# An adaptive-norm transformer block on one core: feed-forward begun inside attention's end, and the key maxima three units ahead of the scores

## The reference

```python
mod = (silu(c) @ wmod).reshape(2, 6, 1, -1)
sa, ca, ga, sb, cb, gb = (mod[:, i] for i in range(6))    # ga, gb: kept at least 0.25 from zero
h = layernorm(x) * (1 + ca) + sa
x = x + ga * attention(h)      # 16 heads of 8; a token sees pages (32 tokens) up to its own
h = layernorm(x) * (1 + cb) + sb
x = x + gb * ffn(h)

# ffn: four rounds r, four experts e, the best two by logits
logits = cur @ Wg[r] + bg[r]
vals, idx = top_k(logits, 2)
cw = sum(one_hot(idx) * softmax(vals))                    # weight of each expert
hmid = gelu(einsum('nh,ehf->enf', cur, W1) + b1)
y = einsum('enf,efh->enh', hmid, W2) + b2
cur = cur + einsum('ne,enh->nh', cw, y)
```

## Time and profile before

| | |
|---|---|
| median of 3 runs | 743.12 us (735.27 to 758.76) |
| profiled execution, its device time | 735.29 us |
| its span | 733.5 us |
| PE / PEld | 661.3 us (90%) / 444.6 us (61%) |
| DVE | 570.4 us (78%) |
| ACT | 518.2 us (71%) |
| POOL | 177.9 us (24%) |
| mean granted clock of TensorE | 0.943 |

### The profile page before, as it was taken

One profiled execution on the slowest core, in us unless ns is written; L12 is line 12 of the kernel. 1 busy time (PEld: TensorE's weight loads), 2 busy tenths in 40 slices (PEclk: granted clock), 3 DMA queues, 4 the chain that ended last, 5 costly groups with the idle time before them and its releaser, 6 DMA issues.

```text
span 733.5 us, 11093 instructions
## 1 busy us (share of the span) xinstructions
PE 661.3 (90%) x4004; PEld 444.6 (61%) x4004; DVE 570.4 (78%) x951; ACT 518.2 (71%) x920; POOL 177.9 (24%) x154
## 2 busy tenths in 40 slices
PE   3936799999999989946999999999999999999996
PEld 2413344444444435535787778777877787778885
DVE  5577878888888864466789888888889888988775
ACT  2420077787787777634888888888888888888983
POOL 0232520000000000003244334442444244422222
PEclk9975589999999999966999999999999999999998
DMA  7288001011101000002111101110111011110200
GB/s 267 83 279 270 2 2 60 18 44 61 40 22 61 3 1 4 1 0 66 50 59 59 56 3 59 58 59 2 57 59 58 12 48 59 59 37 21 74 15 29
DMA packets 16902, 40.64 MB, mean 55 GB/s; under 512 B 2832, under 2 KB 8208, under 8 KB 14736
## 3 DMA queue, kind: packets, MB, share of 16 engines
q1 hardware_dynamic: 15536, 38.20, 15.3%
q10 hardware_dynamic: 1312, 1.74, 0.7%
HBM read 32.19 MB, written 9.57 MB: 57 GB/s over the span
## 4 chain that ended last, share of the span: by engine, by line
PE 35%; DVE 12%; issue 5%; ACT 1%; POOL 0%; POOLq 0%; DVEq 0%
DVE gel_lo L1027 7%; PE y L930 6%; PE y L932 6%; PE y L931 6%; PE hid L921 5%; PE hid L920 5%; PE hid L919 5%; PE plog L941 2%; DVE part L1083 1%; ACT gel_hi L995 1%; DVE at_least L1055 1%; PE pcw L950 1%; DVE cw L1074 0%; DVE cw L1072 0%; DVE dl L1062 0%
## 5 line engine op out<-in xcount | busy, mean ns | idle before, releaser
L1027 DVE TENSOR_TENSOR gel_lo<-gel,gel_hi 128x512 fp32r<-128x512 f32 x256 | 248.3, 1010 | 6.7 <-ACT gel_hi L995 5.7
L567 ACT ACTIVATE probs<-st 128x512 f32<-128x512 f32 (+1 forms) x320 | 160.4, 555 | 95.2 <-PE st L703 91.7
L599 DVE TENSOR_REDUCE mcol<-mx 128x2 f32<-128x1024 f32 (+2 forms) x160 | 176.7, 1118 | 38.5 <-PE mx L722 36.0
L994 ACT ACTIVATE gel<-hid,b_sb 128x512 f32<-128x512 f32 x256 | 176.1, 688 | 39.5 <-PE hid L921 17.1
L995 ACT ACTIVATE gel_hi<-hid,b_sb 128x512 fp32r<-128x512 f32 x256 | 174.8, 683 | 0.0
L1135 POOL TENSOR_TENSOR cur<-cur,part 128x512 f32<-128x512 f32 x64 | 106.5, 1663 | 251.3 <-DVE part L1083 251.3
L722 PE MATMUL mx<-ks,qs 30*128 30x128 f32 (+4 forms) x576 | 90.3, 392 | 22.5 <-PEq L228 13.3
L930 PE MATMUL y<-gel_hi,w_hi 128*128 128x512 f32 x256 | 104.6, 408 | 0.4 <-DVE gel_lo L1027 0.2
L919 PE MATMUL hid<-cur_hi,w_hi 128*128 128x512 f32 x256 | 102.5, 401 | 0.0
L920 PE MATMUL hid<-cur_lo,w_hi 128*128 128x512 f32 x256 | 102.3, 399 | 0.0
L921 PE MATMUL hid<-cur_hi,w_lo 128*128 128x512 f32 x256 | 102.2, 399 | 0.0
(11 more groups left out here) (140 smaller groups left out, 569.1 us busy)
## 6 DMA issues: line engine op xcount, KB each, us to landing
cwb<-gate_rows SPq DMA_DIRECT2D x16, 1024.0 KB, 4.7
ks<-k_rows SPq DMA_DIRECT2D x8, 512.0 KB, 3.7
qs<-q_rows SPq DMA_DIRECT2D x8, 512.0 KB, 4.8
q_rows<-pieces_q SPq DMA_DIRECT2D x12, 256.0 KB, 3.8
k_rows<-pieces_k SPq DMA_DIRECT2D x12, 256.0 KB, 4.5
x_sb<-in_x SPq DMA_DIRECT2D x4, 256.0 KB, 4.8
...
```

The costliest lines, as they stand in the source:

```text
L567: nc.scalar.activation(probs[k % PROBS][:, h, 0:n], st[:, (HG * k + h) % ST_RING, 0:n], ACT.Exp, scale=SCALE).then_inc(exp_done, 1)
L599: nc.vector.tensor_reduce(mcol[g % 2][:, PAIR_HEADS[pair]:PAIR_HEADS[pair] + 2, slot:slot + step * (len(blocks) - 1) + 1:step], mx[:, at % ...
L994: nc.scalar.activation(gel[n % RING][:, :], hid[n % RING][:, :], ACT.Gelu_apprx_tanh, bias=bias)
L1027: nc.vector.tensor_tensor(gel_lo[n % RING][:, :], gel[n % RING][:, :], gel_hi[n % RING][:, :], ALU.subtract).then_inc(lo_ok, 1)
```

## The change

1. `rstd_steps` and `root_step` are gone. `root_guess` (three VectorE instructions) makes a first guess of the inverse root from the bits of the number, and `root_refine` makes three Newton steps, 12 linked instructions, each waiting for the one before. In `prep` both are on VectorE; behind it the refinement and the scaling of the tiles are on GpSimd.
2. `LEAD` is 3 in place of 4, `TURN_AFTER` is one unit in place of two, and four bins change places.
3. Attention projects only 12 of the 16 tiles, with all of it ahead of the last `weigh`, and makes only chunk 0 of the feed-forward's input: GpSimd refines and scales, `normed` stands in the last unit, ScalarE's `hidden` between its exponentials, GpSimd cuts `cur`. It then also refines and scales chunk 1, `norm(1)`, in the same block.
4. The last four tiles, and the input of chunks 1 to 3, are made inside the feed-forward, between its steps 1 and 32, by tables of step numbers. The routing of chunks 0 to 4 has step numbers of its own.
5. `xn`, `rec`, `att`, `att_t` and the pieces of `cur` lie in memory that outlives the block; `cur_hi`, `cur_lo` and `cwb` take the place of `pieces` (so the order listings below name them pieces_q).

```diff
-LEAD = 4
-TURN_AFTER = 2 * PAIRS
+LEAD = 3
+TURN_AFTER = PAIRS
@@ BINS
+    ([(0, 0), (4, 512)], 128, 0, 12),
     ([(1, 0), (5, 512)], 256, 1, 12),
-    ([(0, 0), (4, 512)], 128, 0, 12),
     ([(5, 0)], 512, 5, 1),
+    ([(2, 256), (6, 768)], 128, 10, 4),
     ([(6, 0)], 512, 6, 1),
-    ([(2, 256), (6, 768)], 128, 10, 4),
@@
+def root_guess(nc, link, m, tiles):
+    ve, rstd, nw = m.ve[:, tiles, :], m.rstd[:, tiles, :], m.nw[:, tiles, :]
+    link(nc.vector.tensor_scalar(ve, m.mv[:, tiles, 1:2], EPS, None, ALU.add))
+    link(nc.vector.tensor_scalar(nw.bitcast(I32), ve.bitcast(I32), 1, None, ALU.arith_shift_right))
+    return nc.vector.tensor_scalar(rstd.bitcast(I32), nw.bitcast(I32), -1, ROOT_GUESS, ALU.mult, ALU.add)
+def root_refine(eng, link, m, tiles):
+    for _ in range(ROOT_STEPS):
+        link(eng.tensor_tensor(nw, rstd, rstd, ALU.mult))
+        link(eng.tensor_tensor(nw, nw, ve, ALU.mult))
+        link(eng.tensor_scalar(nw, nw, -0.5, 1.5, ALU.mult, ALU.add))
+        link(eng.tensor_tensor(rstd, rstd, nw, ALU.mult))
@@ attention, gpsimd
+            def norm(c):
+                pool.wait_ge(var_ok, c + 1)
+                root_refine(nc.gpsimd, link, m, chunk_tiles(c))
+                for t in range(TPC * c, TPC * (c + 1)):
+                    scaled(nc.gpsimd, m, xn, t).then_inc(xn_ok, 1)
+            norm(0)
+            pool.wait_ge(h_ok, 1)
+            nc.gpsimd.tensor_copy(m.cur_hi[:, 0, :], m.cur[:, 0, :]).then_inc(hi_ok, 1)
+            pool.wait_ge(hi_ok, 1)
+            nc.gpsimd.tensor_tensor(m.cur_lo[:, 0, :], m.cur[:, 0, :], m.cur_hi[:, 0, :], ALU.subtract).then_inc(cur_ok, 1)
+            norm(1)
@@ attention, tensor
+            for step in range(STEPS - FIRST_TILE, TILES + 2):
+                project(step)
             weigh(STEPS - 1)
-            pe.wait_ge(exp_done, HG * STEPS)
-            for step in range(STEPS - FIRST_TILE, NT + 2):
-                project(step)
-                if step == JB + 5:
-                    normed(0)
-                    normed(1)
-            normed(2)
-            normed(3)
@@ ffn
+    FIRST = 3 * TPC
+    TO_TOKENS = [6, 8, 12, 17]
+    DIVIDE = [7, 9, 13, 18]
+    BACK = [8, 14, 18, 22]
+    TURNED = [9, 15, 19, 23]
+    WO = [10, 16, 20, 24]
+    RESIDUAL = [11, 17, 21, 25]
+    GUESS = 26
+    FIRST_COMBINE = 6
+    NORMED = {1: 1, 2: 10, 3: 31}
+    HIDDEN = {1: 2, 2: 11, 3: 32}
+    START = {0: -1, 1: 4, 2: 15, 3: 33, 4: 44}
+    RANKS, TANH, WEIGHTS = (1, 3, 4, 5), 6, 7
@@ ffn, vector, ahead of step 0
+            for stage in range(len(RANKS)):
+                ranks(0, stage)
             low(0)
+            weights(0)
@@ ffn, gpsimd
+            norm(2)
+            parts(1)
             for k in range(CHUNKS):
                 for e in range(NE):
+                    accumulate(k, e)
+                    if (k, e) == (0, 2):
+                        parts(2)
+                    if (k, e) == (1, 1):
+                        norm(3)
+                if k == 1:
+                    parts(3)
+                    parts(4)
```

346 lines of the change are left out of this document (223 added, 123 removed).

## The result

| | before | after |
|---|---|---|
| median of all runs | 741.41 us (735.27 to 762.14, 20 runs) | 736.6 us (725.72 to 741.13, 20 runs) |
| fastest run | 735.27 us | 725.72 us |
| profiled execution | 735.29 us (span 733.5) | 737.9 us (span 736.1) |

The ratio is 0.9883, 95% interval 0.984 to 0.9926: a little faster, and no difference by the bound of 2%. The forecast was 719 us with a range of 712 to 731. The ratio compares only the runs within 1.5% of each kernel's fastest, and so is nearly blind to what makes the others long; the profiled execution of after isn't one of them, so I read it for its parts, and then look for what sets it apart.

The account below looks back on a forecast made before the run. TensorE was taken to bound the feed-forward by its instruction count, with a 37 us hole ahead of it. First `down` 25.6 us earlier, less 6.3 of work and 3.0 of waits, is 16.3: 735.3 becomes 719 us, range 712 to 731.

Parts of the forecast that it names:

- the scaling of a tile: GpSimd scaling a 128x128 tile at attention's end: 0.4 us each, between 0.21 and 1.26, four tiles 1.6 us.
- Root in prep: In prep, 15 linked VectorE instructions replace a 2.83 us chain and take 3.1 us: a cost of 0.25 us.
- Lead: Bins ahead of the first score: one unit less makes it come 2.1 us sooner, bounds 0.8 and 2.5.
- both at nothing: Later groups and reordered bins: no cost or gain, within 1 us either way for seven groups.
- Attention's end: Last attention unit: GpSimd's chain ends the block, so the feed-forward begins at 312.95 in place of 330.70, bounds 312 and 316.5.
- Start of the feed-forward: From the feed-forward's beginning to its first `down`: 6.7 us, at 319.65, bounds 5.3 and 9.3.
- The full stretch: Feed-forward behind the first `down`: 6.3 us of added TensorE work and 3.0 of new waits, waits' bounds 0 and 7.
- the 1.5 taken: Feed-forward step 31: TensorE stalls 1.5 us because `norm(3)` takes 8.5 us and is awaited 7 us after the guess.
- three signs that the prediction named for being wrong: Scaling a tile takes 1 us or more; `low` releases `down` in most steps to 24; clock under 0.9 behind step 5.
- The rule that I cited: Two-input VectorE instructions lock out GpSimd's SBUF reads: `norm(3)` up to 10 us, a stall of 3; a value between taken.
- the rival of VectorE and GpSimd holding TensorE up: Feed-forward steps 4 to 45: 7 us of stalls, a gain of 9 to 10 us, 725.5 us; chance 0.28.
- the clock stays at half: Behind the feed-forward's stuttering start, half clock for ten steps at 1.1 us more each: gain 5, 730 us; chance 0.07.

Follow-up runs that it names:

- after_again: The changed kernel run once more, unaltered: ratio 0.9882 to the kernel before, median 739.8 us, fastest 727.0.
- lead_only: The kernel before with only the lead of three, the earlier turn and the new order of bins: ratio 1.0019, median 746.5 us against 738.6.
- scale_dve: The changed kernel with the tiles scaled on VectorE in place of GpSimd, refining left on GpSimd: ratio 0.9843 to the kernel before, median 729.2 us.
- normed3_late: The changed kernel with chunk 3's transposes at step 34 in place of 31, its logits and chunk 4's later too: ratio 0.9826 to the kernel before.
- busy_tail: The changed kernel with two extra unread matmuls in each of the first four score units without bins: ratio 0.9852 to the kernel before, median 727.2 us.
- lead_four: The changed kernel with the lead of four, the turn and the order of bins as before: ratio 0.9893 to the kernel before, median 729.0 us.
- scale_busy: The changed kernel with tiles scaled on VectorE and extra unread matmuls in four score units behind the last bins: ratio 0.979 to the kernel before, median 722.6 us.
- combined: The changed kernel with tiles scaled on VectorE, chunk 3's transposes at step 34 and extra matmuls behind the last bins: ratio 0.9799 to before, median 724.9 us.

## Why the prediction was wrong

The step that failed most is a term that the sum put at nothing: the lead's effect on the later groups, where the clock fell. Besides it the scaling of a tile and the work and waits of the full stretch were taken too small. In the sum's order:

**Root in prep: right.** The same place, from `ve` to the copy behind the root, answers to the earlier trace rows, and took 3.13 us in place of 2.83, +0.30 for +0.25:

```profile
10.96 0.17 DVE L179 TENSOR_SCALAR ve<-mv 128x16 f32<-128x16 f32 x1
...
14.09 0.17 DVE L347 COPY modc<-pmod 128x12 f32<-128x12 f32 x1
```

**Lead: right in its price, wrong in "both at nothing".** The first score came 2.04 us sooner behind the first bin (2.1 were taken), released by the same transfer:

```profile
84.26 0.47 PE L727 MATMUL st<-qs,ks 30*128 30x128 f32 x2 [0.59 <-DMA qs<-mrow]
```

What failed is the sentence that the reordered bins and the later groups cost nothing, which I checked for waits only, with no term for the clock. A unit of bins less ahead of the scores moves the end of the bins a unit later, and the projection's first step with it, onto other units. In the two units between them TensorE has gaps. Before they lay ahead of the last turn, and now the turn lies between them; and in the second the clock falls. The granted clock of the 2.7 us behind the last turn is 0.64, 0.67, 0.80, 0.67 and 0.67 in after, after_again, lead_only, scale_dve and normed3_late, and 1.00 in the other nine: so it falls in all five profiles that have this lead without extra matmuls, in none of the five that have it with them, and in none of the four with the lead of four. The price is 9.3 us in the profiled execution (51.33 against busy_tail's 42.03 from the last turn to the logits), 7.8 to 15.4 in the four others (each against the run with the same end of the block and the extra matmuls), and by the medians 7.6 us (lead_four) to 9.4 (busy_tail), which were taken on another chip. **This is the largest part of the gain that went missing**: from 719 us to the median of 736.6 it is 17.6 us, of which the other terms make 5.9 (10.4 in place of 16.3); the 11.7 left are the clock's, here and in the first group, which a median doesn't tell apart. The fastest runs, at the highest mean clock (0.951), show the change without the fall, 9.5 us under before.

**Attention's end: right chain, one term too small.** From `to_tokens` of unit 79 to the logits 10.93 us for 9.75. The scaling of a tile was taken at 0.4 us inside 0.21 to 1.26; it is 0.785. On four tiles that is 1.5 us. Moving it to VectorE gave just that back: 9.42 us in scale_busy. The value should have been taken nearer the wide instruction.

**Start of the feed-forward: right in size, by another path.** 7.03 us for 6.7. The ranking, 329.12 to 331.74, took 2.6 us where 3.3 were taken, so GpSimd's short instructions beside it cost less, and the weights were ready at 332.96. But the turn stands behind four ups on TensorE, and these ended only then, at half clock: TensorE was busy for 7.06 of the 7.10 us at a clock of 0.50. The prediction put these ups (5 us) beside its chain; with the logits' 1.84 ahead of them they are as long as the chain, and here they set the time. That the number came out is luck.

**The full stretch: two terms too small.** 14.2 us for 6.3 + 3.0. TensorE's busy time grew by 8.2 us (103.22 against 95.05), its idle time by 6.0 (7.1 against 1.05). In the 8.2 stand some 1.2 us of half clock (0.98 against 0.99 in the mean); the other 7.0 are the work for which 6.3 were taken, 0.7 too little. Behind the 6.0 stand the waits listed above, 6.8 in all: 2.9 on `norm(3)` for the 1.5 taken, since TensorE came to step 31 sooner than the 7 us allowed for, 5.9 behind the guess. (That `norm(3)` took 8.7 us for 8.5 is luck in part: 5.1 undisturbed and 3.4 for collisions were taken, and it was 6.6, with the tiles at 0.785, and 2.1.) The others are 1.9 on `low` and 1.2 on the weights, 0.8 on the last residual. The direction of each was forecast, and the places; of the stall's price I left out what follows it: the clock's fall, and a GpSimd that comes late to its next cuts. normed3_late shows the whole price, 3.7 us less than after_again. None of the three signs that the prediction named for being wrong came: a tile took 0.785 us and not 1, `low` released `down` late 4 times in 64 steps, and the clock behind step 5 was 0.98.

**The rule that I cited, and the sum.** At steps 48 and 49 the trace of combined shows VectorE and GpSimd side by side. GpSimd, then VectorE (POOL L1298 is the cut, L1306 `accumulate`; DVE L1135 is `low`, L1161 and L1163 are short ranking instructions of 0.22 us by themselves):

```profile
405.87 1.67 POOL L1306 TENSOR_TENSOR cur<-cur,part 128x512 f32<-128x512 f32 x1 [4.67 <-DVE part L1191]
...
408.31 1.27 POOL L1298 TENSOR_TENSOR pieces_q<-cur,pieces_q 128x512 fp32r<-128x512 f32 x1
```

```profile
406.31 1.31 DVE L1161 TENSOR_TENSOR at_least<-at_least,tri 128x64 f32<-128x64 f32 x1
...
407.79 0.52 DVE L1163 TENSOR_TENSOR at_least<-at_least,above 128x64 f32<-128x64 f32 x1
408.34 1.78 DVE L1135 TENSOR_TENSOR gel_lo<-gel,gel_hi 128x512 fp32r<-128x512 f32 x1
...
410.58 0.69 DVE L1135 TENSOR_TENSOR gel_lo<-gel,gel_hi 128x512 fp32r<-128x512 f32 x1
```

A `low` that begins with the cut ends as much later as the cut is long, less 0.2: 1.78 in place of 0.69. A ranking instruction beside `accumulate` takes 1.31 in place of 0.22. The Trainium skill, "SBUF — State Buffer", section "Who interferes with whom", calls it an exclusive lock, and these rows agree. For the full stretch I had applied it only to GpSimd's side, where it stands for the difference between 6.6 and 8.7 us of `norm(3)`; VectorE pays too, and its `low` is what `down` waits for (from `down` 49 to 50 it took 3.23 us here, 1.7 of them the longest of the waits on `low`). The trace of before had this price: the ranking of chunk 0, which took 5.9 us with GpSimd's cuts beside it and 2.5 without.

**Altogether.** With the measured terms and no fall of the clock the sum is -10.4 us, 724.9 us, which is where the fastest runs of the changed kernel lie (725.7), and near what the rival of VectorE and GpSimd holding TensorE up gives (725.5; its own terms, 16.3 less 4, 1.7 and 1.7, add up to a gain of 8.9 and 726.4), by other terms. With the fall in most runs the median is 736.6. The rival "the clock stays at half" had the right subject at the wrong place: I looked for it behind the hole, where it was up after `down` 0, and not in the first group and in attention's last stretch, which I had called busy. The sum also starts from an execution whose first group was the shortest of the fourteen, 24.02 us.

**What stays open.** Why two thin units ahead of the turn leave the clock up (in before and lead_four), and one on either side of it not, no row shows: the gaps are 0.68 or 0.69 us in both. Lead, turn and order of the bins were always changed together, so which of the three opens the place isn't shown either. In the first group the clock rises at some point from 95 to 131 us: where it rose 8 us behind the first score (before at 97, scale_busy at 95) the group took 24.0 and 24.1 us, and where it rose 44 us behind it (lead_only, 131) 34.8. At 14 to 15 us the group took 26.6 to 26.8 with either lead, so its length is the moment of the rise and not the lead's own work; and that moment isn't the same in two executions of one kernel (109 in after, 100 in after_again). The group took 28.4 us in the mean of the ten profiles with the lead of three and 25.8 in the four with four; whether the lead makes the rise later or chance does, they don't settle. More work for TensorE ahead of it didn't bring the rise forward. In how many runs the last fall comes, and whether it visits the kernel before and lead_four too, the runs don't settle.
